# Moving the Q, K and V evictions from ScalarE to VectorE, and spreading small constant work, in a fused attention and feed-forward layer

## The reference, cut to what matters

```
xn = layernorm(x)                       # 16 x 2048 x 1024, per token
Q, K, V = xn @ Wq, xn @ Wk, xn @ Wv     # 1024 -> 128
attn = softmax(causal(Q K^T / sqrt(128))) @ V
h = xn @ W1 + b1                        # 1024 -> 4096
q = h + (cos(th) wr + sin(th) wi) * wi * sin(th + 0.1 h) * 0.1
y = x + attn @ Wo + relu(q) @ W2 + b2
```

## Time and profile before

| | us |
|---|---|
| median of 3 runs | 1227.78 |
| fastest of them | 1227.72 |
| the profiled execution's own time | 1227.48 |
| its span on core 0, the slowest | 1225.8 |
| spans of the 8 cores | 1219.6 to 1225.8 |

### The profile page before, as it was taken

One profiled execution on the slowest core, in us unless ns is written; L12 is line 12 of the kernel. 1 busy time (PEld: TensorE's weight loads), 2 busy tenths in 40 slices (PEclk: granted clock), 3 DMA queues, 4 the chain that ended last, 5 costly groups with the idle time before them and its releaser, 6 DMA issues.

```text
span 1225.8 us, 23745 instructions; the slowest of 8 cores (1219.6 to 1225.8 us)
## 1 busy us (share of the span) xinstructions
PE 1079.9 (88%) x7810; PEld 737.4 (60%) x7936; DVE 453.6 (37%) x1007; ACT 595.0 (49%) x1285; POOL 37.0 (3%) x48
## 2 busy tenths in 40 slices
PE   2757474779999999999999999999999999999997
PEld 2745463456665666666656665666566656666665
DVE  3535553543333333333333333333333333333333
ACT  3945494534454544454445454545444545444443
POOL 1310031000000000000000000000000000000000
PEclk9967696679999999999999999999999999999999
DMA  8889578920202020202020202020202030203010
GB/s 191 234 139 165 164 226 144 175 85 1 86 3 86 1 87 1 87 1 86 2 87 2 87 1 87 2 86 2 87 1 87 1 86 1 87 1 87 6 48 36
DMA packets 47416, 87.13 MB, mean 71 GB/s; under 512 B 7106, under 2 KB 23490, under 8 KB 46274
## 3 DMA queue, kind: packets, MB, share of 16 engines
q1 hardware_dynamic: 36226, 59.39, 16.0%
q0 software_dynamic: 11072, 26.22, 12.0%
HBM read 78.25 MB, written 25.17 MB: 84 GB/s over the span
## 4 chain that ended last, share of the span: by engine, by line
PE 72%; issue 2%; DVEq 2%; DVE 2%; ACT 1%; ACTq 0%
PE psOut L831 36%; PE psW L805 36%; DVEq L751 2%; DVE probs L753 1%; ACT rb_sb L778 1%; DVE u_sb L730 1%; DVE out_sb L753 0%; PE psOut L821 0%; DVEq L758 0%; DVEq L729 0%; DVEq L750 0%; DVEq L727 0%; ACTq L777 0%; ACTq L775 0%; ACT ss_sb L770 0%
## 5 line engine op out<-in xcount | busy, mean ns | idle before, releaser
L805 PE MATMUL psW<-xn_r,W_sb 128*128 128x256 bf16 x4096 | 538.3, 275 | 1.5 <-PEq L385 1.5
L831 PE MATMUL psOut<-W_sb,rb_sb 128*128 128x512 bf16 x1936 | 515.3, 383 | 16.1 <-ACT rb_sb L778 10.2
L805 PEld LDWEIGHTS psW<-xn_r,W_sb 128*128 128x128 bf16 x4096 | 404.5, 99 | 161.9 <-issue 5.6
L730 DVE SCALAR_TENSOR_TENSOR u_sb<-ss_sb,Rp_sb,psW 128x256 f32<-128x256 bf16 x512 | 244.3, 480 | 584.7 <-ACT ss_sb L770 571.8
L770 ACT ACTIVATE ss_sb<-psW,phb_sb 128x256 bf16<-128x256 f32 x512 | 242.1, 473 | 444.1 <-PE psW L805 444.1
L831 PEld LDWEIGHTS psOut<-W_sb,rb_sb 128*128 128x128 bf16 x2048 | 200.7, 99 | 150.5 <-issue 19.7
L778 ACT ACTIVATE rb_sb<-u_sb,b_sb 128x256 bf16<-128x256 f32 x511 | 254.5, 498 | 57.2 <-DVE u_sb L730 55.1
L590 DVE CAST pT_big<-psT 128x512 bf16<-128x512 f32 (+2 forms) x80 | 48.9, 612 | 42.6 <-PE psT L525 38.4
L525 PE MATMUL psT<-diag_li,xn_rg 128*128 128x128 bf16 x272 | 33.2, 272 | 24.1 <-DVE pT_big L590 14.9
L369 PE MATMUL psTx<-diag_li,probs 128*128 128x128 bf16 x176 | 15.3, 238 | 38.4 <-DVE diag_li L274 38.3
L539 PE MATMUL psO<-pT_big,V_tm 128*128 128x128 bf16 x272 | 32.0, 265 | 16.5 <-DVE pT_big L590 16.0
(11 more groups left out here) (92 smaller groups left out, 428.5 us busy)
## 6 DMA issues: line engine op xcount, KB each, us to landing
x_sb<-x SPq DMA_DIRECT2D x52, 512.0 KB, 5.8
W_sb<-w POOLq DMA_DIRECT2D x8, 2048.0 KB, 41.4
xn_scr<-xn_rg POOLq DMA_DIRECT2D x32, 256.0 KB, 4.3
xn_r<-xn_scr SPq DMA_DIRECT2D x16, 512.0 KB, 8.0
out<-out_sb SPq DMA_DIRECT2D x32, 256.0 KB, 3.6
out<-probs SPq DMA_DIRECT2D x32, 256.0 KB, 6.0
xn_r<-x SPq DMA_DIRECT2D x12, 512.0 KB, 5.7
Q_fm<-b2rep SPq DMA_DIRECT2D x1, 512.0 KB, 4.3
```

The costliest lines, as they stand in the source:

```text
L730: su2.inc(v.scalar_tensor_tensor(u2_sb[ci % 2][:], ss_sb[ci % 2][:], Rp_sb[:, c:c + 1], psW1[slot][:], ALU.mult, ALU.add))
L805: ins = t.matmul(psW1[slot][:], W1_sb[:, k * DFF + c * 128: k * DFF + (c + 1) * 128], xn_r3[g % 2][:, k * R3:(k + 1) * R3], start=(k == 0) ...
L831: ins = t.matmul(psOut[tt][:, h * 512:(h + 1) * 512], rb_sb[cw % 3][:, tt * 128:(tt + 1) * 128], W2_sb[:, cc * D + h * 512: cc * D + (h + ...
```

## The change

- In the QKV stage of both sequences the Q, K and V copies (three of 512 columns, four times) leave ACT's order and enter DVE's: behind the diagonal of tiles 4, 8 and 12, and once more at the end. In front of them DVE waits for q(4r-1) (`sqk`) and drains. ACT keeps its own wait for the same q before it copies T(4r).
- In the second sequence's attention stage `vops` is dealt out three entries to each of tiles 0 to 8 and one to tile 9, instead of four to each of tiles 0 to 6. `_mid` moves from tile 9 to tile 13 and `_tail` from tile 12 to tile 15. On ACT the sign moves from step 8 to step 12 and the arctangent from step 11 to step 14.

```diff
@@ vector, QKV stage @@
                             sdg3.inc(ins)
+                            if jj >= 4 and jj % 4 == 0:
+                                rp = jj // 4 - 1
+                                v.wait_ge(sqk.h, sqk_b + 4 * (rp + 1))
+                                v.drain()
+                                sqke.inc(v.tensor_scalar(
+                                    Q_fm[:, rp * R1:(rp + 1) * R1], psQ[:],
+                                    QSCALE, None, ALU.mult))
+                                sqke.inc(v.tensor_copy(
+                                    K_fm[:, rp * R1:(rp + 1) * R1], psK[:]))
+                                sqke.inc(v.tensor_copy(
+                                    V_tm[:, rp * R1:(rp + 1) * R1], psVB[:]))
+                    rp = NR1 - 1
...
@@ scalar, QKV stage @@
-                            if tt == 0 and r >= 1:
-                                rp = r - 1
-                                sc.wait_ge(sqk.h, sqk_b + 4 * (rp + 1))
-                                sqke.inc(sc.activation(Q_fm[:, rp * R1:(rp + 1) * R1],
-                                                       psQ[:], AF.Copy, scale=QSCALE))
-                                sqke.inc(sc.copy(K_fm[:, rp * R1:(rp + 1) * R1], psK[:]))
-                                sqke.inc(sc.copy(V_tm[:, rp * R1:(rp + 1) * R1], psVB[:]))
...
@@ attention stage @@
-                        pv.setdefault(min(i // 4, 6), []).append(fn)
+                        pv.setdefault(min(i // 3, 9), []).append(fn)
...
-                    pv.setdefault(9, []).append(_mid)
+                    pv.setdefault(13, []).append(_mid)
...
-                    pv.setdefault(12, []).append(_tail)
+                    pv.setdefault(15, []).append(_tail)
...
-                        if s == 1 and qq == 8:
+                        if s == 1 and qq == 12:
                             sc.wait_ge(sp2.h, 1)
...
-                        if s == 1 and qq == 11:
+                        if s == 1 and qq == 14:
                             sc.wait_ge(sp2.h, 2)
```

More of the change, by code:

```diff
@@ L278, in _ @@
                             sdg3.inc(ins)
+                            if jj >= 4 and jj % 4 == 0:
[10 more added lines that the diff above has]
+                    rp = NR1 - 1
+                    v.wait_ge(sqk.h, sqk_b + 4 * (rp + 1))
+                    v.drain()
+                    sqke.inc(v.tensor_scalar(Q_fm[:, rp * R1:(rp + 1) * R1],
+                                             psQ[:], QSCALE, None, ALU.mult))
+                    sqke.inc(v.tensor_copy(K_fm[:, rp * R1:(rp + 1) * R1], psK[:]))
+                    sqke.inc(v.tensor_copy(V_tm[:, rp * R1:(rp + 1) * R1], psVB[:]))
                     v.drain()
```

## The result

| | us |
|---|---|
| predicted (range) | 1240 (1231 to 1247) |
| after, median of 9 runs | 1247.17 |
| before, median of 10 runs beside them | 1228.41 |
| ratio, with its 95% interval | 1.0153 (1.0142 to 1.0164) |
| spans of the 8 cores, before and after | 1219.6 to 1225.8, and 1239.8 to 1246.3 |

The change costs 18.8 us, 1.5%. I had forecast 12.6 us, so the direction was right and the size was not; the time lies just outside the range.

A forecast was written before the change was run, and what follows sets the result against it. The prediction took the loop between PE and the copies, not ACT's load, to set a QKV round. It summed 2 x 2.0 + 7 + 1.6 = +12.6 on 1227.48 us to 1240, range 1231 to 1247.

The forecast's parts named there:

- order of the QKV stage: QKV stage, both sequences: longer rounds and a later last copy on DVE start attention later, +2.0 us a sequence.
- clock: QKV stage: matmuls run at half speed behind PE's longer gaps, +7 us over both sequences.
- attention: Second sequence's attention stage: moved constants gain 3.2 us, the arctangent's wait for `_mid` turns this into +1.6 net.
- The loop that sets a round: QKV stage: PE waits for V's copy, the next copies wait for q(4r-1); this, not ACT's load, sets a round.
- full clock: QKV stage, rival: no slow gaps, matmuls stay at full clock; 1233 us, chance 0.17.
- nothing moves: Rival: fewer copies on ACT and a longer round cancel, with the arctangent's wait small; 1228 us, chance 0.07.
- faster: QKV stage, rival: q(4r-1) is done when DVE gets there, a round takes 9.3 us; 1219 us, chance 0.05.
- the arctangent's wait: Attention, second sequence, rival: `_mid` comes early enough to cover it, attention gains 3.2 us; 1235 us, chance 0.10.
- 1.4 a gap: QKV stage: half speed behind a longer PE gap makes 1.6 us late, less 0.2 for DVE's diagonals running ahead.
- five of six: QKV stage: of six PE gaps over both sequences, five are followed by half speed, +7 us; all six +8.4.
- the cover is gone: End of QKV stage: the last store had covered 1.2 us of ACT's end; now DVE ends at 71.8, store 71.5.
- much slower: QKV stage, rival: TensorE drops to half clock and stays, +21 us a sequence; 1272 us, chance 0.06.

The follow-up runs named there:

- e5_filled_gap: The changed kernel with 64 extra matmuls on PE ahead of T(5), T(9) and T(13), its psTx buffer wait moved ahead; 1237.21 us, ratio 1.0064.
- e2_attn_only: The changed kernel with the Q, K and V copies put back on ACT, so only the attention part is changed; 1231.62 us, ratio 1.0021.
- e1_qkv_only: The changed kernel with the attention stage put back as before, so only the copies on DVE are changed; 1245.23 us, ratio 1.0135.
- e6_wait_only: The changed kernel with the copies left on ACT, but DVE's wait for q(4r-1) and its drain kept; 1231.57 us, ratio 1.0027.
- e3_copies_later: The changed kernel with wait and copies one tile further down DVE's order, behind the diagonal of tile 4r+1; 1225.71 us, ratio 0.9967.
- e8_last_twice: The changed kernel with only the last round's three copies of each sequence made twice; 1249.24 us, ratio 1.0159.

## Why the prediction was wrong by size, step by step

Predicted: order of the QKV stage 4.0, clock 7, attention 1.6, together 12.6. Measured, by the ratios: order 7.9 - 2.6 = 5.3 (`e5_filled_gap` above before, less `e2_attn_only`), clock 18.8 - 7.9 = 10.9, attention part 2.6. The first two are uncertain by some 3 us; the table of stages, which compares single executions, gives 5.7 and 11.5. So of the 6.2 us of the miss 3.9 are the clock's, 1.3 the order's and 1.0 the attention part's.

*Right.* The loop that sets a round, the place of the wait in it and every term of the round's sum: 11.7 with full clock, 4.16 us of gap where 4.1 was worked out, 0.60 a copy, the first Q copy 0.17 us behind the end of q(3) instead of 1.11, so 0.94 earlier where I had 0.9. With the copies in that place the relief of ACT was worth nothing. All five rivals fell: full clock was not kept, the rounds of 13.1 to 13.8 leave no room for "nothing moves" or "faster", half clock did not stay, and the arctangent's wait was not covered.

*Wrong: "1.4 a gap", and "five of six".* This term is the largest miss, 3.9 of the 6.2 us. I took the length of the slow stretch from the earlier trace rows, where it lasted some 3 us behind a gap of 2.49, and priced three groups of matmuls at half speed. Behind the gaps of 4.16 it lasted up to 5.0 us (40.83 to 45.8), six groups at 0.83 instead of 0.45: 6 x 0.38 = 2.3 late, of which DVE's lead takes 0.25. That leaves 2.05; rounds with the shorter slow stretch (about 3.5 us) cost 1.4. By the table of stages the mean is 11.5 / 6 = 1.9. The rounds show the two sizes: 13.1 and 13.7 to 13.8, against 11.7 at full clock. And all six gaps were followed by it, not five. On no core of before did a slow stretch last longer than 3.9 us, so another core's rows would not have shown it. A row behind a shorter gap was a lower bound for the price, and I had used it as the price, so the range was too low as well: it took in a sixth slow gap, but no longer slow stretch.

*Wrong: the tail, from the last Q copy to attention.* I had it shrink from 2.92 to 2.1 us (69.9 to 72.0), with "the cover is gone". It came out as 3.7 and 3.0 (means), 0.7 longer in the first sequence and unchanged in the second. Against the forecast that is 1.5 + 0.8 = 2.3 more, enough for the whole miss in the order's term (5.3 or 5.7 against 4.0). The step that failed is "the store, issued behind T(15)'s copy at about 67.8": I put the issue at the end of ACT's copy. The rows of after say otherwise:

```profile
74.81 1.01 ACT L328 CAST xn_rg<-psTx 128x1024 bf16<-128x1024 f32 x1 [0.96 <-PE psTx L375]
```

```profile
76.82 0.84 POOL L232 DMA_DIRECT2D xn_scr<-xn_rg  x1 [1.59 <-ACT xn_rg L328]
```

```profile
DMA to landing us min/median/max: 4.8/4.8/4.8
```

```profile
82.17 0.27 PE L509 MATMUL psLogA<-K_fm,Q_fm 128*128 128x128 bf16 x1 [4.70 <-PEq L184]
```

The copy ends at 75.82, POOL issues at 76.82, the data land 4.8 later at 81.62, and attention starts at 82.17. Two microseconds of DVE lie beneath that. The row to use stood ahead of the prediction: before, the store was issued at 66.2 and the last Q copy began at 67.07, 0.9 apart, and both hang from the same T(15). In after they are 0.8 apart (76.82 and 77.63). I had also misread how long the landing takes: the 3.7 that I used is the larger of the two in the earlier trace rows and belongs to the store of tile 14. The store of tile 15 alone, in before:

```profile
L232 POOL DMA_DIRECT2D xn_scr<-xn_rg x1: 844/844/844, 66.2 to 66.2; - x1
DMA to landing us min/median/max: 3.3/3.3/3.3
```

It landed at 69.5, and attention started 0.5 behind it. With these rows the forecast would have been 69.9 - 0.9 + 3.3 + 0.5 = 72.8, a tail of 2.9, and that is what the second sequence shows (3.0). The first is longer because its last store took 3.2 to 4.8 us to land, by core, where before it took 3.2 to 3.4; why is not shown. I had written that I would be wrong if the barrier were still set by the store alone; it was.

*Attention: right to 0.1 in its stage, in part by luck, and missed beside it.* The stage grew by 1.5, with +1.6 forecast. Inside it, the constants of tiles 0 to 6 gave 2.0 (forecast 1.8). Tiles 7 to 9 took 1.1 (0.6). Tiles 9 to 13, without the arctangent and `_tail`, gave 2.9 (2.0). The new wait made DVE's step from tile 13 to 14 longer by 5.8, as worked out (2.6 + 3.2), and the last two tiles gave 0.4 back. So the moves ahead of the wait gave 3.8 instead of 3.2, DVE came to tile 14 some 2.0 late instead of 2.6, and 1.5 of that was left at the end, where PE was to absorb 1.0 of the 2.6: misses that cancel. "The last stage keeps its length" did not hold: it was 0.4 to 0.9 us longer in the runs that carry the attention part, `e2_attn_only` (960.1) among them, and not in `e1_qkv_only` (959.3). On core 0 of after its first 24 matmuls run at full speed, in 2.8 us instead of 4.5, and then a slow stretch comes behind the first group boundary (clock 0.83 from 346 to 356 us) instead of the second. I have no run that changes only this, so its cause stays open.

One slip stands in a rival that did not come true: for "much slower" 67 us against 44 make +23 a sequence and not +21, so some 1276 and not 1272.

## What to carry to other kernels

On an engine that runs in order, work moved off a busy engine carries its wait along: look for what stands behind that wait, and who needs it next. The same copies one tile later, behind the diagonal that PE waits for, turned a loss of 16.6 us into a gain of some 6; no busy share told the two apart. And price a pause of TensorE with the slow matmuls behind it, from a pause of at least that length; if the trace has none, take the one there is as a lower bound and widen the range upward.

## What the runs showed of the hardware that I had not expected

- Half speed (1.2 GHz) lasted 2.8 to 5.3 us behind a gap of 4.16 (mean 4.7), and 2.7 to 6.1 behind one of 5.95 (mean 4.6). It cost 1.4 to 2.05 us net a gap, besides the gap itself. Behind gaps of 2.87 in `e6_wait_only` it came in 24 of 39 cases, behind shorter ones less often: nine times on the eight cores of before, behind gaps of 1.4 to 2.5, and on three cores once in `e3_copies_later`, behind gaps of 1.4.
- Matmuls that nobody needs paid: 64 of them in each of six gaps gave back 10.9 us of 1247 (`e5_filled_gap`), even with a stretch of 14 us on two of the eight cores in which eight matmuls took 0.70 instead of 0.61.
- The landing of a 256 KB store took 3.2 to 4.8 us, and the next stage's first matmul came 0.50 to 0.63 behind it on every core, before and after. With the change it put attention's first matmul 1.0 to 2.65 us behind DVE's last copy, where 0.69 us was enough once DVE came last (`e8_last_twice`).
